# Graph layer on one core: own rows scaled on ACT, value rows added by an accumulating DMA of GpSimd

## The reference, cut to what matters

```python
Q = relu(x @ Wq + bq)
V = x @ Wv + bv
# _gcn: coef = dinv[src] * dinv[dst], dinv = 1/sqrt(degree)
gcn = segment_sum((x @ Wg)[src] * coef, dst) + bg
# _former: Q normalised and rectified, turned by cos/sin of an angle per node
out = cosQ @ (cosQ.T @ V) + sinQ @ (sinQ.T @ V)      # over a norm per node
out = layer_norm(out / norm + gcn + V, gamma, beta)
result = layer_norm(x + relu(out))
```

## Time and profile before

| what | value |
|---|---|
| median of 3 runs | 1887.72 us (1881.73, 1887.72, 1896.17) |
| profiled execution, its own time | 1891.69 us |
| its span | 1889.8 us |
| granted TensorE clock, mean | 0.942 of 2.4 GHz |
| PE busy | 1642.4 us (87%) |
| DVE busy | 1585.2 us (84%) |
| ACT busy | 953.7 us (50%) |
| POOL busy | 1038.4 us (55%) |
| DMA, mean | 229 GB/s |

### The profile page before, as it was taken

How to read it: one execution, slowest core, us unless ns; L and a number is a source line. 1 busy time by engine, 2 the same in 40 slices (tenths; PEclk the granted TensorE clock), 3 DMA queues, 4 the chain that set the end, 5 groups by cost and what they waited for, 6 DMA issues and landing times.

```text
span 1889.8 us, 27579 instructions
## 1 busy us (share of the span) xinstructions
PE 1642.4 (87%) x7707; PEld 1252.9 (66%) x7707; DVE 1585.2 (84%) x4322; ACT 953.7 (50%) x1789; POOL 1038.4 (55%) x1106
## 2 busy tenths in 40 slices
PE   5888974999999997788888879999899898988995
PEld 4566652777777775565556667767677776777774
DVE  7999975899889897787777878888689888887886
ACT  2222213555555555555555556656456555554554
POOL 0000006777777777677787758878445444444440
PEclk8999985999999999899999989999899898998998
DMA  6445578899888998677777858878566676675762
GB/s 218 160 159 176 173 271 267 281 307 302 290 289 304 302 302 264 196 233 231 247 237 238 246 185 258 257 246 269 167 202 206 197 220 197 195 210 167 220 189 88
DMA packets 179601, 433.16 MB, mean 229 GB/s; under 512 B 24558, under 2 KB 26218, under 8 KB 179432
## 3 DMA queue, kind: packets, MB, share of 16 engines
q0 software_dynamic: 71120, 233.10, 41.0%
q1 hardware_dynamic: 87180, 159.65, 24.8%
q10 hardware_dynamic: 21132, 38.50, 5.5%
HBM read 354.13 MB, written 77.03 MB: 228 GB/s over the span
## 4 chain that ended last, share of the span: by engine, by line
DVE 37%; PE 31%; DMA 11%; issue 7%; ACT 6%; POOL 5%; SPq 1%; DVEq 1%; ACTq 0%; POOLq 0%
DVE stage L787 7%; PE bank L1104 6%; PE bank L1105 6%; PE bank L1106 6%; PE bank L1188 5%; DMA rows<-scaled_g,index_slots 5%; DMA split<-scaled_g,index_slots 5%; PE bank L1190 5%; DVE split L832 4%; POOL split L441 3%; DVE rows L832 3%; DVE stage L783 3%; ACT split L518 3%; DVE one_hot L828 2%; DVE stage L1046 2%
## 5 line engine op out<-in xcount | busy, mean ns | idle before, releaser
L441 POOL DMA_INDIRECT split<-scaled_g,index_slots x490 | 531.5, 1085 | 334.1 <-PE bank L1190 212.4
L441 POOL DMA_INDIRECT rows<-scaled_g,index_slots x392 | 423.8, 1081 | 174.3 <-PE bank L1190 80.0
L1188 PE MATMUL bank<-split,one_hot 128*128 128x512 f32 x882 | 380.5, 431 | 120.4 <-DVE split L832 62.8
L518 ACT CAST split<-split 128x512 fp32r<-128x512 f32 x490 | 301.3, 617 | 356.1 <-PE bank L1190 185.5
L832 DVE TENSOR_TENSOR split<-split 128x512 fp32r<-128x512 f32 x490 | 336.8, 687 | 86.1 <-ACT split L518 84.4
L518 ACT CAST split<-rows 128x512 fp32r<-128x512 f32 x392 | 240.7, 617 | 275.7 <-PE bank L1190 177.2
L1104 PE MATMUL bank<-weights,operands 128*128 128x512 f32 x784 | 323.4, 412 | 4.2 <-DMA operands<-turned_x 4.2
L1188 PEld LDWEIGHTS bank<-split,one_hot 128*128 128x128 f32 x882 | 170.3, 193 | 233.7 <-DVE rows L832 109.0
L1106 PE MATMUL bank<-weights,operands 128*128 128x512 f32 x784 | 317.3, 405 | 0.0
L1105 PE MATMUL bank<-weights,operands 128*128 128x512 f32 x784 | 316.9, 404 | 0.0
L832 DVE TENSOR_TENSOR rows<-rows,split 128x512 fp32r<-128x512 f32 x392 | 270.0, 689 | 50.9 <-ACT split L518 49.3
(11 more groups left out here) (201 smaller groups left out, 2553.9 us busy)
## 6 DMA issues: line engine op xcount, KB each, us to landing
turned_x<-operands SPq DMA_DIRECT2D x49, 512.0 KB, 3.0
operands<-turned_x SPq DMA_DIRECT2D x49, 512.0 KB, 5.9
stage<-values SPq DMA_DIRECT2D x98, 256.0 KB, 4.1
stage<-in_x SPq DMA_DIRECT2D x96, 256.0 KB, 2.7
scaled_g<-nodes SPq DMA_DIRECT2D x49, 256.0 KB, 3.4
own_rows<-scaled_g SPq DMA_DIRECT2D x49, 256.0 KB, 4.1
values<-stage ACTq DMA_DIRECT2D x49, 256.0 KB, 4.1
combine<-values SPq DMA_DIRECT2D x49, 256.0 KB
```

The lines of the kernel that those rows point to most:

```text
L441: pool.indirect_dma_start(out=plain(row_ring[k % RING]), out_offset=None, in_=table, in_offset=bass.IndirectOffsetOnAxis(ap=index_slots[:, ...
L518: act.copy(hi_ring[k % SPLIT], plain(row_ring[k % RING])).then_inc(s["chunk_rounded"], 1)
L1188: pe.matmul(gcn_banks[seq % 2][:, :], one_hot[:, slot, :], hi_ring[slot], start=k == 0, stop=False, skip_group_check=True)
```

## The change

`combine_load` and its waits are gone from SP's list, and `add_own` from DVE's. ACT now scales the own rows in place (`scale_own`, an activation with `dinv` as the scale of each partition) after chunk 6 of the tile's round, when `own_rows` has landed. After the 18 gathers of the tile POOL waits for this and for the tile's value rows to be stored, and issues a DMA that adds the rows of `values` onto `own_rows` in SBUF. `combine_tile` reads the neighbour sum and `own_rows`, and writes `combine`; it waits for the accumulating DMA (`values_added`) and for the last store from `combine`. `own_load` waits for `combine_tile` of the tile before instead of `add_own`.

```diff
@@ sync @@
             def own_load(seq):
-                sp.wait_ge(s["own_added"], freed(seq, 1))
+                sp.wait_ge(s["gcn_combined"], freed(seq, 1))
                 sp.dma_start(own_rows[:, :], dram_rows(table, seq, P)).then_inc(s["own_loaded"], 16)
-            def combine_load(seq):
-                sp.wait_ge(s["combined_stored"], seq * 16)
-                sp.dma_start(combine[:, :], dram_rows(values, seq, P)).then_inc(s["combine_loaded"], 16)
...
@@ gpsimd, gather_tile, behind the 18 gathers @@
+                pool.wait_ge(v_stored[seq % QV_STEPS], seq // QV_STEPS * 16 + 16)
+                pool.wait_ge(s["own_scaled"], done(seq))
+                pool.dma_start(own_rows[:, :], dram_rows(values, seq, P), accum_op=ALU.add)\
+                    .then_inc(s["values_added"], 16)
                 with pool.If(surplus > 0):
...
@@ constants @@
+    OWN_AT = 6
...
@@ scalar @@
+            def scale_own(seq):
+                act.wait_ge(s["own_loaded"], seq * 16 + 16)
+                act.activation(own_rows[:, :], own_rows[:, :], ACT.Copy, scale=column(dinv, seq))\
+                    .then_inc(s["own_scaled"], 1)
...
                     chunk(i, k)
                     if k == 3:
                         store_combined(i - 1)
+                    if k == OWN_AT:
+                        scale_own(i)
...
@@ vector @@
-            def add_own(seq):
-                dve.wait_ge(s["combine_loaded"], seq * 16 + 16)
-                dve.wait_ge(s["own_loaded"], seq * 16 + 16)
-                dve.scalar_tensor_tensor(combine[:, :], own_rows[:, :], column(dinv, seq), combine[:, :],
-                                         ALU.mult, ALU.add).then_inc(s["own_added"], 1)
...
             def combine_tile(seq):
                 if exists(seq):
-                    dve.wait_ge(s["own_added"], done(seq))
+                    dve.wait_ge(s["values_added"], seq * 16 + 16)
+                    dve.wait_ge(s["combined_stored"], seq * 16)
                     dve.wait_ge(s["gcn_summed"], done(seq))
-                    dve.scalar_tensor_tensor(combine[:, :], gcn_banks[seq % 2][:, :], column(dinv, seq), combine[:, :],
+                    dve.scalar_tensor_tensor(combine[:, :], gcn_banks[seq % 2][:, :], column(dinv, seq), own_rows[:, :],
                                              ALU.mult, ALU.add).then_inc(s["gcn_combined"], 1)
...
                 if k == 1:
                     combine_tile(seq - 1)
-                if k == 16:
-                    add_own(seq)
```

More of the change, by code:

```diff
@@ L180, in build_layer @@
             "setup_done", "pads_set", "dst_loaded", "src_loaded", "bias_loaded", "g_x_turned",
-            "g_scaled", "table_written", "own_added", "own_loaded", "combined_stored",
-            "combine_loaded", "m_split", "v_kept", "q_biased", "rows_bias_loaded",
+            "g_scaled", "table_written", "own_scaled", "own_loaded", "combined_stored",
+            "values_added", "m_split", "v_kept", "q_biased", "rows_bias_loaded",
             "moment_split", "o_turned", "consts_set", "columns_ready", "chunk_indexed", "extra_indexed",
@@ L311, in own_load @@
             def own_load(seq):
-                sp.wait_ge(s["own_added"], freed(seq, 1))
+                sp.wait_ge(s["gcn_combined"], freed(seq, 1))
                 sp.dma_start(own_rows[:, :], dram_rows(table, seq, P)).then_inc(s["own_loaded"], 16)
-            def combine_load(seq):
-                sp.wait_ge(s["combined_stored"], seq * 16)
-                sp.dma_start(combine[:, :], dram_rows(values, seq, P)).then_inc(s["combine_loaded"], 16)
-            def v_is_stored(i):
-                sp.wait_ge(v_stored[0], i * 16 + 16)
-                sp.wait_ge(v_stored[1], i * 16)
-                sp.wait_ge(v_stored[2], i * 16)
             for i in range(0, QV_LOOPS - 1):
                 own_load(i)
-                x_load((i + 1) * QV_STEPS, 0)
-                v_is_stored(i)
-                combine_load(i)
-                x_load((i + 1) * QV_STEPS + 1, 1)
-                x_load((i + 1) * QV_STEPS + 2, 2)
+                for j in range(QV_STEPS):
+                    x_load((i + 1) * QV_STEPS + j, j)
             own_load(QV_LOOPS - 1)
             x_load(FULL, 0)
-            v_is_stored(QV_LOOPS - 1)
-            combine_load(QV_LOOPS - 1)
             own_load(QV_LOOPS)
-            v_is_stored(QV_LOOPS)
-            combine_load(QV_LOOPS)
             def v_load(g, slot, t):
@@ L354, in v_loads @@
                             own_load(i + seq0)
-                        if j == steps - 1:
-                            combine_load(i + seq0)
                         v_load(i * steps + (1 + j + sweep * TILES), (1 + j + sweep) % 2, i * steps + (1 + j))
@@ L384, in out_round @@
                 for j in range(OUT_STEPS):
-                    if j == 2:
-                        combine_load(i + OUT_SEQ)
                     out_loads(i, j, P)
@@ L465, in _ @@
             for name in ("g_x_hi", "g_kept", "chunk_rounded", "q_rect", "q_root",
-                         "q_kept", "m_hi", "o_hi", "o_root1", "o_root2", "o_scaled2"):
+                         "q_kept", "m_hi", "o_hi", "o_root1", "o_root2", "o_scaled2", "own_scaled"):
                 act.sem_inc(s[name], LEAD)
@@ L605, in m_rounds @@
                             store_combined(i + (seq0 - 1))
+                        if k == OWN_AT:
+                            scale_own(i + seq0)
                         for j in range(steps):
@@ L650, in out_round @@
                         store_combined(i + (OUT_SEQ - 1))
+                    if i < OUT_LOOPS and k == OWN_AT:
+                        scale_own(i + OUT_SEQ)
                     for n, j, at in in_flight(k, i, OUT_STEPS, 4):
@@ L685, in _ @@
             link = linked("dve_chain", 0, 0)
-            for name in ("g_x_split", "bins_ready", "chunk_split", "own_added", "gcn_combined",
+            for name in ("g_x_split", "bins_ready", "chunk_split", "gcn_combined",
                          "v_kept", "q_biased", "q_stats", "q_scaled", "m_split", "o_split", "o_norm_ready",
```

## The result

The changed kernel takes 1902.06 us (median of 15 runs, 1896.13 to 1907.81), the kernel before in the same series 1886.02 (15 runs, 1878.62 to 1896.17). The ratio is 1.0085, 95% interval 1.0067 to 1.0103: 16 us slower, where I had forecast 33.7 and a median of 1921. The sign and the range (1900 to 1970) held, the size did not: less than half of the forecast loss came.

What follows compares the result with a forecast made beforehand. POOL was taken to bound COS and SIN, POOL and PE together QV, and mostly DVE's lines OUT. POOL's DMA +39.0 and DVE's relief -5.3 gave +33.7 us: 1921 us, 1.8% slower, range 1900 to 1970.

Steps and rivals of the forecast that it cites:

- DVE's relief: Dropping add_own pays in OUT only: 60% of 8.9 us, -5.3 us; nothing in QV, COS and SIN.
- Faster: Rival: POOL's DMA nearly free, DVE's relief remains in OUT and perhaps QV; -10 to -20 us, about 1870; chance 0.07.
- POOL's DMA: 34 added DMAs in QV, COS and SIN cost 47.6 us, less 6.2 true waits and 2.4 cushion: +39.0 us.
- The load of V: Load queued behind own_load: ACT waits 1 or 2 us in SIN, hidden in gather waits; 0, otherwise 16 us.
- POOL's instruction near 1.1 us: Sign: POOL's new line shows a mean near 1.1 us in QV, COS and SIN.
- COS rounds: Sign: rounds of COS at 29.2 instead of 27.7 us.
- ACT waits for gathers in QV: Sign: in QV ACT waits for gathers too, no longer mainly for PE.
- the combination at k = 1 never waits: Sign: DVE's combination has no idle time ahead; the DMA has 8.3 us to land.
- ACT's scaling free: ACT's added 0.72 us activation a tile stands beside its waits: cost nothing, without that cover 35 us.
- QV's rounds: Sign: rounds of QV at 27.5 to 28 instead of 26.6 us; keeping 26.6 would show the forecast wrong.
- the DMA is slow: Rival: the add lands at 8.8 us or later, DVE waits at k = 1; 1938 to 2047 us; chance 0.11 beyond the range.
- QV swallows it: Rival: POOL's DMA costs nothing in QV, where PE is as full; +12 to +19.5 us, 1900 to 1907; chance 0.16.

Runs made afterwards that it cites:

- e15: Changed kernel with a DVE pass over a same-size buffer put back at k = 16, its result unused: 1.0173 against the kernel before.
- e12: The changed kernel measured again, nothing altered, on one chip with three others: 1.0084 against the kernel before.
- e3: Kernel before without DVE's add_own pass, own rows left out of the result: 0.9895 against the kernel before, -20 us.
- e11: Kernel before without DVE's add_own pass in QV only (own rows left out there): 0.9961 against the kernel before, -7 us.
- e0: The kernel before run again, unaltered, for a profile beside others: 1.0009, QV window 434.3 us.
- e2: Kernel before plus one plain POOL DMA a tile, 256 bytes of each of 128 rows into an unread buffer: 1.0064, +12 us.
- e10: Changed kernel without POOL's accumulating DMA (value rows left out) and with own_load behind the second load of V: 0.9909 against the kernel before.
- e4: Changed kernel with a plain POOL DMA in place of the accumulating one (scaled own rows overwritten): 1.0071 against the kernel before.
- e13: Repeat of the changed kernel with own_load behind the second load of V in COS and SIN: 1.0066 against the kernel before.
- e9: Changed kernel's new way in QV and OUT, the kernel before's way in COS and SIN: 0.9984 against the kernel before.
- e1: Changed kernel with own_load moved behind the round's second load of V in COS and SIN: 1.0075 against the kernel before.
- e8: Changed kernel with own_load behind the second load of V and ACT's scaling at chunk 8 instead of 6: 1.0140 against the kernel before.
- e6: Changed kernel without ACT's scaling, own rows added unscaled: 1.0123 against the kernel before.
- e14: Repeat of the new way in OUT alone, other stages as in the kernel before: 0.9931, 1872.5 us against 1882.9.

## Why the prediction was wrong, point by point

**The step that failed: DVE's relief at -5.3 us, counted in OUT alone because "in QV PE and POOL are full".** The relief is worth 17 to 20 us (e15 against e12, e3 against before): each is known to 7 to 10 us, and both lie above the 8.9 that I had as the bound. Of that some 11 are QV's (9.5 us of 15 rounds in e11, for 17 tiles) and some 9 OUT's: the mean OUT window with a pass, e0, e2, e11, e15 and before, is 436.2, without it 428.4, 7.8 us over 10 rounds or 0.78 a tile, about the pass's full 0.74 of the earlier trace rows, though it is known only to some 5 us. I took 60% of it in OUT because the chain also runs over PE's lines, and no row gave that share; and I took zero in QV because the row sums left POOL no free time. But these sums show only that POOL's instructions fill the round, not that they would fill a shorter one. POOL in QV, groups by line, e10:

```profile
L418 POOL DMA_INDIRECT split<-scaled_g,index_slots x151 | 153.0, 1013 | 45.5 <-issue 23.2 <-POOL index_slots L413 8.2 <-PE bank L1171 7.4
L418 POOL DMA_INDIRECT rows<-scaled_g,index_slots x120 | 128.7, 1072 | 38.8 <-issue 25.6 <-PE bank L1171 4.3 <-POOL index_slots L413 4.1
```

By the same sum POOL is full again in e10 (84.3 us idle for 271 gathers at 0.30), yet the window is 9.6 us shorter than the earlier trace rows: its gathers sum to 281.7 us in place of 288.2. POOL's busy time in QV is 310.0 and 308.6 us with the pass, 302.7 and 301.0 without (e10, e11). So in these profiles POOL's instructions stretched with the round, and the engine that looked full wasn't the only one that set it. What stretches them is not shown: in the kernel before, gathers that lie beside L839 have a median of 947 ns, no longer than the others (956), and e0, whose QV is slow, has 301.6 us of POOL with the pass. PE's waits give the hint I had passed over; of the kernel before in QV, and of e10:

```profile
PE bank L1188 <- DVE rows L832: 8.0, 19, 1.6
```

```profile
PE bank L1169 <- DVE rows L821: 3.1, 4, 1.1
```

19 waits in 15 rounds, about one a tile, were for DVE; without the pass there are 4. Of PE's idle time for DVE in the kernel before, 5.0 us lie in the last 2 us ahead of the combination, behind `add_own` (which starts 4.6 us ahead of it); in e10 it is 0.9 us, in e11 1.5. But these waits are a part only. PE's idle time in the window falls from 10.1 to 7.4 us, and its busy time from 388.4 to 381.5 us (380.3 in e11) with the same 1637 or 1638 instructions. Part of that is the clock: TensorE was at 1.2 GHz for 9.6 us of the window before, for 3.4 us in e10 and never in e11, which makes up to 4.8 of the 9.5 us, and the 6.2 us of it at the window's very start need not be the pass's doing. The total of e11, -7 us (0 to -14), is in line with either reading. My rival "Faster" had the price for QV, "up to 16 x 0.74 = 11.8 if PE's short waits are for DVE", but tied it to a nearly free DMA.

**POOL's DMA, +39.0 us: right in its direction and place, too large in price.** I priced it as a gather and its 0.30, 1.36 to 1.44 us. It has no 0.30 ahead of it, and of its 1.02 us only 0.60 hold up the next instruction; with the copy behind it, which becomes longer, POOL loses the 1.0 to 1.1 us a tile that were read off between two tiles (e4 above). By my own formula that is 16 x 1.0 + 18 x 1.1 - 6.2 - 2.4 = +27. The windows say a little more: QV 12.9 us over 15 rounds (401.9, the mean of changed, e12, e13 and e9, against 389.0), which is 14 for 16 tiles; COS 9.8 over 10 rounds (287.5 against 277.7), 11 for 11 tiles; SIN 5.9 over 6 (e1, e2, e8, e13 against the eight without), 7 for 7 tiles. (COS goes by nine windows with the DMA, and eight without it and without the late load.) That is +32; by the totals, e13 against e10, it is +30, known to some 8. I can't tell 27 from 32. What part of it is POOL's instruction and what part the data is open. e4 leaves little for the add: -3 us without it, known to some 7. But e2's plain DMA of 32 KB took 0.7 to 0.9 us a tile from POOL, for which my formula gives some 20 us, and cost 12. Beside DVE's pass and the early load it differs from e4 in the bytes (32 KB for 256), in having nothing to wait for on ACT, and in its group's long QV, in which POOL has room by the same sum; a plain DMA of 256 KB in the kernel before would tell, and wasn't run.

**The load of V, 0 us: wrong.** I had written "a wait of 1 or 2 us, which hides in ACT's waits for gathers. If not, 16 us". It is 2.9 us on average (17.6 over 6) and 4.0 at most in SIN. The windows give 4.7 us over 6 rounds (178.8 with it, 174.1 without), some 6 for SIN, and that includes TensorE's lower clock behind many of these waits, which the prediction had no term for (SIN 0.95 to 0.97 with the late load, 0.99 to 1.00 without). In COS ACT never waited for the load, as forecast. The total of e13 against e12 shows 3.4 and can't tell 0 from 11.

**The sum anew:** 30 to 32 for the DMA, -17 to -20 for the relief, +3 for the load give +13 to +18; measured were +16.0. Each term is known to 7 us or so at best, so that the middle comes out right is luck.

**What held, and what didn't.** POOL's instruction near 1.1 us by the record (1.02); COS rounds 28.9 for the forecast 29.2; ACT waits for gathers in QV; the combination at k = 1 never waits; OUT shorter by most of 0.74 us a round and more; ACT's scaling free as far as e6 shows, which gained nothing without it. QV's rounds did not hold: 26.7 us (400.3 over 15) for the forecast 27.5 to 28, which the prediction had named as a sign that it is wrong. Of the rivals, "the DMA is slow" fell: it lands after 5.4 us at the median and 7.6 at most in the first profile (9.5 once in e12), within the 8.3 that DVE has, and not after 8.8. By the Trainium skill's "Collectives: The Full Stack", section "The bandwidth ceiling: the fold count and why AG ≠ RS ≠ AR", the add would halve the rate; here it took 5.4 us in place of 4.4 for the plain DMA of e4. By the Trainium skill's "SBUF — State Buffer", section "A bandwidth-pool intuition that's wrong (but worth ruling out)", a DMA of GpSimd beside a DVE copy takes some 3.1 us; this trace has 1.12 at most. "QV swallows it" would have been read as true from the changed kernel's profile alone, QV being only 1.8 us longer, and the measured 1902.06 us lie in its 1900 to 1907. It is false: QV pays some 11 to 16 us for the DMA, and DVE's relief pays most of them back (e10, e13, e14, e15).

## What to carry to other kernels

An engine whose instructions and idle times add up to the round need not set the round: look also for short waits that come once a tile, and take the suspected pass out on the chip before counting its removal at nothing. A change that moves work from one engine to another is better tried stage by stage: here it costs where the receiving engine is the late one, pays in the one stage where it has room (OUT alone, 0.9931), and a stage that doesn't move can be two effects of some 12 us each. When an entry in a queue of DMAs is given a later event to wait for, ask what stands behind it: here the one that came late was its successor, and TensorE's clock fell behind the wait. Look also at how far the profiled execution lies from the median of its runs before its windows are used as a price.

## What the hardware showed that I had not expected

- The accumulating DMA of GpSimd has 1016 ns at the median in the record, the plain one of the same 256 KB 595 ns, and that of 32 KB in the same 128 rows 593: the record's length doesn't depend on the bytes. In COS the next instruction of POOL starts 0.6 us after either, so the record by itself is no price. Between two tiles of COS POOL lost 1.1 us with the add and 0.8 without it, in QV 1.0 and 0.9.
- A direct DMA of POOL starts with no idle time ahead of it (median 0 in the changed kernel), where each indirect one has at least 0.27 us, 0.30 at the median.
- Adding in flight made the transfer land 1.0 us later (5.4 against 4.4 us for 256 KB), not twice as late.
- POOL's unchanged instructions in QV took 310 and 309 us with DVE's pass (before, e14) and 303 and 301 without it (e10, e11); but e0 has the pass, a slow QV, and 302 us.
- Idle stretches of TensorE of 2.8 to 3.4 us were each followed by 3.4 us at 1.2 GHz instead of 2.4 (SIN of the changed kernel, five times in six rounds); in e4 it was three of six.
